# Three input groups of a DSS/FP4 kernel scaled or split at other places on ScalarE, in the set-up and steps 0 and 1

## What is computed

```python
xn = layernorm(x)                       # over the 256 channels
k  = dss_kernel(...)                    # a filter of 128 taps per channel
s  = causal_conv(xn, k) + xn * D
gate = fp4_linear(xn, w_gate)           # 256 -> 704, blocks of 16 rounded to FP4
y    = fp4_linear(xn, w_up)
h    = silu(gate) * y
g    = silu(fp4_linear(h, w_down))      # 704 -> 256
out  = x + s * g
```

## Time and profile before

| | us |
|---|---|
| three runs | 580.74, 582.33, 582.70 |
| their median | 582.33 |
| the profiled execution, its own time | 582.21 |
| its span | 580.4 |

### The profile page before, as it was taken

The page is one execution under the profiler, slowest core; times in us unless marked ns, Lnnn a source line. Parts: engine busy times, 40 slices in busy tenths (PEclk is TensorE's granted clock), DMA queues, the critical chain, the costliest instruction groups (busy, mean ns, idle before and its releaser), DMA issues.

```text
span 580.4 us, 13234 instructions
## 1 busy us (share of the span) xinstructions
PE 476.4 (82%) x4956; PEld 332.1 (57%) x4956; DVE 539.3 (93%) x681; ACT 409.5 (71%) x576; POOL 203.9 (35%) x304
## 2 busy tenths in 40 slices
PE   0000376679999999999999999999999999998975
PEld 0000343235555567777777777777777777775654
DVE  6999998899999999999999999999999999998883
ACT  6945897898888877676666667676767676764543
POOL 1493001754545551111111111333333333147860
PEclk9999857889999999999999999999999999999988
DMA  6990012242222345353535353435353535339978
GB/s 174 349 286 0 2 36 92 92 99 93 90 91 92 110 128 154 100 153 102 147 101 150 102 148 104 149 96 156 99 158 95 161 96 159 96 62 155 171 103 129
DMA packets 101186, 70.80 MB, mean 122 GB/s; under 512 B 8848, under 2 KB 100752, under 8 KB 101008
## 3 DMA queue, kind: packets, MB, share of 16 engines
q1 hardware_dynamic: 93072, 61.94, 36.4%
q0 software_dynamic: 8064, 8.13, 9.6%
HBM read 61.28 MB, written 16.91 MB: 135 GB/s over the span
## 4 chain that ended last, share of the span: by engine, by line
PE 58%; DVE 25%; issue 7%; POOL 4%; ACT 3%; DMA 0%; SPq 0%; DVEq 0%; POOLq 0%
PE ps L1236 28%; PE ps L1254 10%; PE ps L1256 5%; PE ps L1245 5%; PE ps L1269 4%; PE ps L1273 4%; DVE wgu L978 4%; DVE sm L831 2%; DVE work L889 2%; POOL gbuf L522 2%; PE ps L1224 2%; DVE work L884 2%; DVE work L915 2%; DVE xh L956 1%; DVE work L850 1%
## 5 line engine op out<-in xcount | busy, mean ns | idle before, releaser
L1236 PE MATMUL ps<-wgu,work 128*128 128x512 f16 (+1 forms) x1152 | 245.0, 368 | 16.1 <-DVE work L915 14.9
L1236 PEld LDWEIGHTS ps<-wgu,work 128*128 128x128 f16 x1152 | 110.5, 99 | 128.6 <-issue 19.1
L629 ACT ACTIVATE work<-ps,con 128x704 f32<-128x704 f32 x64 | 54.2, 848 | 96.6 <-PE ps L1236 96.6
L1254 PE MATMUL ps<-wdh,work 128*128 128x256 f16 x704 | 88.5, 275 | 5.5 <-ACT gbuf L633 4.7
L624 ACT COPY work<-ps 128x1408 f16<-128x1408 f16 x64 | 84.8, 1327 | 2.2 <-PE ps L1245 1.9
L1254 PEld LDWEIGHTS ps<-wdh,work 128*128 128x128 f16 x704 | 65.8, 98 | 13.7 <-issue 5.3
L884 DVE SCALAR_TENSOR_TENSOR work<-work 128x960 f32<-128x960 bf16 (+2 forms) x67 | 72.1, 1113 | 1.6 <-ACT work L644 1.5
L522 POOL TENSOR_TENSOR gbuf<-gbuf,xh 128x256 f32<-128x256 f32 (+1 forms) x42 | 41.0, 1048 | 91.9 <-DVE work L897 77.8
L889 DVE SCALAR_TENSOR_TENSOR work<-work 128x1920 f16<-128x1920 bf16 (+3 forms) x36 | 69.7, 1936 | 1.2
L850 DVE TENSOR_TENSOR work<-work,ps 128x960 f32<-128x960 f32 (+2 forms) x63 | 68.4, 1126 | 1.1
L831 DVE TENSOR_REDUCE sm<-work 128x120 f32<-128x1920 f32 (+2 forms) x32 | 66.4, 2074 | 1.3
(11 more groups left out here) (155 smaller groups left out, 676.2 us busy)
## 6 DMA issues: line engine op xcount, KB each, us to landing
work<-kpad SPq DMA_DIRECT2D x64, 512.0 KB, 3.8
work<-L_attn_u SPq DMA_DIRECT2D x33, 256.0 KB, 3.4
gbuf<-u_rev SPq DMA_DIRECT2D x4, 2048.0 KB, 18.7
out<-gbuf POOLq DMA_DIRECT2D x7, 1024.0 KB, 10.3
out<-L_attn_u SPq DMA_DIRECT2D x1, 768.0 KB, 5.5
out<-gbuf POOLq DMA_DIRECT2D x1, 768.0 KB, 7.8
work<-L_ffn_w_down SPq DMA_DIRECT2D x1, 704.0 KB, 6.7
work<-L_ffn_w_gate SPq DMA_DIRECT2D x1, 640.0 KB, 4.5
```

What stands on the lines that cost most here:

```text
L1236: last = T.matmul(p_gu[:, a:b], xT[par][:, t, c, :], wgu[:, part, c % 2, a:b], start=(n == 0), stop=(n == len(todo) - 1))
L1254: T.matmul(dst, hT[t][:, c, :], wdh[:, c, :], start=(c == 0), stop=False)
```

## The change

Three places on ACT, nothing else. `a_scale(0)` moves from step 0 into the set-up, ahead of `square(-1, ...)`. In step 0 `a_high(0)` moves ahead of the second `silu_gate`. `a_scale(13)` moves from behind step 1 into step 1, ahead of its second `silu_gate`. The counts that `a_high` waits for are kept. DVE, PE, POOL and SP keep their instructions and their order.

```diff
-            def step(it, par, ..., td1=True, first=True):
+            def step(it, par, ..., td1=True, first=True, more=None):
...
                 if xn:
                     x_norm(it + 3, 1 - par)
+                if a2:
+                    scaled = it + 7 if isinstance(it, int) and it < 2 else it + (NT // 8 + 1)
+                    if not first:
+                        a_high(it * 2, scaled)
+                if more is not None:
+                    a_scale(more)
                 if gu:
                     silu_gate(it * 2 + 1)
                 if td:
                     h_copy(it * 2 - 3, 1)
                 if a2:
-                    if not first:
-                        a_scale(it * 2)
-                    scaled = it + 7 if isinstance(it, int) and it < 2 else it + (NT // 8 + 1)
-                    a_high(it * 2, scaled)
+                    if first:
+                        a_high(it * 2, scaled)
                     a_high(it * 2 + 1, scaled)
...
             for k in range(2):
                 nc.scalar.copy(dn_hi[k], dn_src).then_inc(w_h, 1)
+            a_scale(0)
             square(-1, 0, True, False, 0)
...
-                step(it, it % 2, True, it >= 1, True, True, it >= 1, it >= 2, a2=True, td1=it >= 3, first=it >= 1)
+                step(it, it % 2, True, it >= 1, True, True, it >= 1, it >= 2, a2=True, td1=it >= 3, first=it >= 1,
+                     more=13 if it == 1 else None)
                 if it == 1:
-                    for n in range(6, 8):
-                        a_scale(2 * n + 1)
+                    a_scale(15)
```

More of the change, by code:

```diff
@@ L657, in y_copy, with step @@
                                      scale=con[:, C_CONV:C_CONV + 1]).then_inc(cv_e, 1)
-            def step(it, par, x, xt, xn, gu, ch, td, a2=False, cv=0, c0=None, td1=True, first=True):
+            def step(it, par, x, xt, xn, gu, ch, td, a2=False, cv=0, c0=None, td1=True, first=True, more=None):
                 if td:
```

## The result

| us | kernel before | changed kernel |
|---|---|---|
| median of 8 runs | 581.54 (580.16 to 582.77) | 578.57 (578.34 to 579.89) |
| profiled execution, its own time | 582.21 | 579.55 |
| its span | 580.4 | 577.8 |

The ratio is 0.9955, 95% interval 0.9938 to 0.9973: 2.6 us faster, 1.6 to 3.6. (The medians lie 3.0 us apart. Measured again (first experiment), the changed kernel took 580.07, ratio 0.9976 (0.9961 to 0.9992). The two intervals meet between 0.9961 and 0.9973, a gain of 1.6 to 2.3 us.

The account below looks back on a forecast made before the run. DVE, 93% busy, sets the pace from 127 us, later PE; only waits on ACT before that can be won. Terms 0 + 0 - 1.97 us took the median 582.33 to 580.4, forecast as 580.3, range 579.0 to 582.1.

Parts of the forecast that it names:

- `a_scale(0)` at nothing: Set-up: four scales, 2.0 us, fit into ACT's 2.42 us of idle time, 0.4 us to spare, cost nothing.
- `a_high(0)` at nothing: Step 0, ahead of the second silu gate: the 1.05 us high part fits 1.14 us of ACT idle time, cost nothing.
- the clock rival: Steps 0 to 2: PE's clock rises or falls elsewhere, gain only 1.2 us, time about 581.1; chance 0.17.
- POOL's low parts from 101.8 and tables done at 109.2: Steps 0 and 1: low parts start at 101.8, not 105.49; tables start 3.6 us earlier and end at 109.2.
- `h_parts` at 114.45: Step 1 on DVE: L923 starts at about 114.45, not 116.31, its 1.68 us wait gone; DVE 1.86 us ahead.
- The scales ahead of the gate at 115.2: Step 1: `a_scale(13)`, 2.0 us, fits ACT's 2.53 us idle time; step 2's first gate starts at 123.2, not 125.20.
- `h_mult` of step 2 at 124.1: Step 2: `h_mult` starts at 124.1, not 126.09, 1.97 us earlier, with PE's end as a bound at 1.86.
- No DVE instruction was held by the moved low parts: Around step 0: earlier low parts cost DVE nothing; rival "Slower" had one hold L831, 583.8 us, chance 0.05.
- The shift unchanged at 515: Late steps: the 2.0 us shift at 127 us should still be there at 515, else the gain was given back.
- 1 us for how medians of three runs scatter: Whole kernel: allowance in the range for scatter of three-run medians; the runs shown span 2 us.
- a product of step 2 at half clock: Step 2: a product keeping half clock ends 1.7 us late, ACT's slack takes most, 0.6 us is lost: 580.9.
- given back later: Last stages: something keeping its own time swallows the 2 us, time 582.3; chance 0.10 together with no effect.

Follow-up runs that it names:

- first experiment: The changed kernel run once more with no edit, beside the kernel before: 580.07 us, 12 runs, ratio 0.9976.
- the held pair: Second try: kernel before and changed kernel, both with small matmuls sized to PE's idle gaps to hold its clock: 580.36 us (ratio 0.9985) and 578.11 us (0.9949).
- the held kernel before: Kernel before plus small matmuls in PE's idle times (55 behind step 1's product, 30 more ahead of step 30): 580.36 us, ratio 0.9985.

## Why the prediction was right and wrong

*The steps of the sum.* `a_scale(0)` at nothing: right, 0.44 us to spare where 0.4 was said. `a_high(0)` at nothing: right only against the profile it was priced on. In the changed kernel's own profile PE's product ended at 100.33, so the high part held the gate 0.7 us (101.10; 100.39 with the high part late) and `h_mult` 0.4 us (101.97 and 101.60), as the clock rival had it (0.8 at most). POOL's low parts from 101.8 and tables done at 109.2: 101.73 and 108.99. `h_parts` at 114.45, 1.86 us earlier: 114.73, 1.58 earlier, as PE's product of step 1 ran at half clock here and the gate at 108.45 made `h_mult` 0.3 us late. The scales ahead of the gate at 115.2, which were to fit into 2.53 us of idle time: PE's product ended at 114.01, so they held the gate 0.8 us, to 114.83; ACT still had 0.35 us to spare at the next gate, and it cost nothing. `h_mult` of step 2 at 124.1, 1.97 earlier: 124.21, 1.88, with PE's product as the later of the two, which is the bound of 1.86 that was named. No DVE instruction was held by the moved low parts: L836 took 2.15 us. The shift unchanged at 515: right to 0.02 us.

*The step that failed* is the allowance for PE's clock, and with it the range: the rival "The clock falls otherwise (about 581.1)" and "1 us for how medians of three runs scatter". I let the clock only take from the gain and put all of its effect at steps 0 to 2. The runs showed that it also gives, and that it has three places on the path: steps 0 to 2, step 30 (1.4 us between two executions of one kernel, 534.48 against 533.11 for one `h_mult`), and the last stage, where it gave 0.65 us in the profiled pair. Within steps 0 to 2 the rival's price was too low as well: a product of step 2 at half clock was to cost 0.6 us, and the one at 123.93 took away 1.35 (the shift against the kernel before fell from 3.20 at 130.57 to 1.85 at 146.25). The base moved too, and that goes with the clock: of the 75 runs of the kernel before that stood beside the experiments, without one of 769.82 us, all 46 below 581.55 us have a mean granted clock of 0.968 to 0.974, and 26 of the 29 above have 0.965. The profile that the prediction was read from is of the upper kind (582.21, 0.965). The kernel before fell from 582.33 to 581.54 when there were eight runs, so a forecast of 2 us below the first median stood 0.8 us too high. With the base of eight runs and the sum of the prediction the result would be 579.6, 1 us above what was measured; twelve more runs gave 580.07, which lies inside the range. On which side of 579.0 a median falls is so in part a matter of luck.

*The size.* 1.97 us is right for the pair of profiles it was made on, in which both kernels had a product of step 1 and one of step 2 at half clock (granted clock 0.52 from 104 to 106 us in the changed kernel, 0.50 from 110 to 112 us before). That part of the agreement is luck: with the clock held in one profile of each, the change is worth 1.2 us at step 3 and 1.0 at the end. The gains measured in this study, from median to median, are 1.1 (580.07, beside 581.14), 2.3 (both with small matmuls) and 3.0 us. That the large gain of the first measurement is the change's own is not supported by the held pair's profiles; how often each case comes up is open.

*What stays open.* Where the clock falls in the slower runs of the held kernel before; its only profile was of a fast one. I did not try to raise the clock of the product of step 0 (95.94 in the changed kernel). The rival "given back later" fell as a mechanism of its own: behind step 2 no trace of the changed kernel loses more than 0.2 us except beside a product at half clock.

## What to carry to other kernels

Two moves that are each worth next to nothing can be worth 1 to 2 us together, when two engines' paths meet at one instruction: list, for that instruction, the time at which each of its inputs is ready, and shorten all that are late. When a run-to-run scatter is as large as the expected gain, find its places in two profiles of one kernel before pricing a change, and let it move the forecast both ways. A move into an idle gap that ends with another engine's work is free only in the executions in which that engine is as late as in the profile.

## What the runs showed of the hardware

PE's clock fell in different places in different executions of one program on the same data: the product of step 30 took 3.73 us in the first profile of the changed kernel (granted clock 1.00 from 528 to 532 us) and 5.06 in the second (0.60). The Trainium skill, TensorE: Matmul & The Clock Gate, section What's actually happening, has the watch over PE free-running, not reset when a kernel starts; that the places differ agrees with it. With 55 small matmuls without a reader in a gap the next product took 3.73 us, with 20 in the same gap 6.67. These are single executions: the changed kernel without any, idle for 2.37 us there, had 3.73 us in one profile (117.30) and 5.25 in the other (118.04).

DVE and POOL blocked each other in both directions. POOL's L494 took 2.00 us beside DVE's L889 and 0.19 elsewhere; DVE's L884 took 1.44 us behind a low part and 1.53 behind POOL's L504, against 1.15 alone, while the reduction L831 or L836 took 2.15 beside a low part and without one. The Trainium skill, SBUF — State Buffer, section Who interferes with whom, gives this split between DVE instructions with two SBUF inputs and others; the traces agree.
